# First sum over the edges: two products of constants behind every chunk's product on TensorE

## The reference, cut to what matters

```
agg = jax.ops.segment_sum(x[nbr], dst, num_segments=n)
cnt = jax.ops.segment_sum(jnp.ones((nbr.shape[0],), x.dtype), dst, num_segments=n)
mean = agg / jnp.maximum(cnt, 1.0)[:, None]
return x @ W1.T + b1 + mean @ W2.T + b2
```

## Time and profile before

| | us |
| --- | --- |
| median of 3 runs | 3077.75 (3067.9 to 3085.03) |
| the profiled execution: its own time | 3073.24 |
| its span, first to last instruction | 3071.5 |
| PE busy | 2177.0 (71%) |
| DVE busy | 1633.8 (53%) |
| ACT busy | 1448.1 (47%) |
| POOL busy | 1399.4 (46%) |
| mean granted clock of PE | 0.823 of full |
| the first sum's loop, first gather to last addition | 348.2 to 1034.0, some 22% of the span |

### The profile page before, as it was taken

The page is one execution under the profiler, slowest core; times in us unless marked ns, Lnnn a source line. Parts: engine busy times, 40 slices in busy tenths (PEclk is TensorE's granted clock), DMA queues, the critical chain, the costliest instruction groups (busy, mean ns, idle before and its releaser), DMA issues. The chain is left out here.

```text
span 3071.5 us, 60350 instructions
## 1 busy us (share of the span) xinstructions
PE 2177.0 (71%) x15045; PEld 1791.5 (58%) x15046; DVE 1633.8 (53%) x4124; ACT 1448.1 (47%) x3571; POOL 1399.4 (46%) x1397
## 2 busy tenths in 40 slices
PE   4889744445444589999657677777777598859991
PEld 3756432333332479999535566666666477639990
DVE  8899722222222643333455555655655787873436
ACT  6789622323232343433364444444444588643335
POOL 0000365656565223333135555555655199735550
PEclk9989966767676789999877777777887699979995
DMA  2300154323232511111315555555656288572223
GB/s 100 126 15 22 53 171 135 116 83 89 83 90 82 129 46 34 38 36 36 113 67 172 166 176 166 170 177 169 182 175 160 72 275 268 177 277 87 70 68 135
DMA packets 182513, 368.87 MB, mean 120 GB/s; under 512 B 30426, under 2 KB 67716, under 8 KB 182126
## 3 DMA queue, kind: packets, MB, share of 16 engines
q1 hardware_dynamic: 118489, 208.65, 20.0%
q0 software_dynamic: 53760, 148.67, 18.1%
q10 hardware_dynamic: 10133, 9.97, 1.0%
HBM read 275.35 MB, written 91.83 MB: 120 GB/s over the span
## 5 line engine op out<-in xcount | busy, mean ns | idle before, releaser
L830 POOL DMA_INDIRECT weightsL_w<-y_gnn,all_slot_dst x440 | 421.6, 958 | 408.1 <-PEq L899 158.4
L830 POOL DMA_INDIRECT scores_rows<-h_gnn,all_slot_dst x440 | 430.5, 978 | 370.3 <-ACT scores_ends L2131 230.5
L920 PE MATMUL sum_ps<-weightsL_w 128*128 128x256 f32 x880 | 316.8, 521 | 346.9 <-issue 218.2
L920 PEld LDWEIGHTS sum_ps<-weightsL_w 128*128 128x128 f32 x880 | 214.9, 260 | 448.8 <-issue 412.7
L935 DVE TENSOR_TENSOR sums_acc<-sums_acc,sum_ps 128x256 f32 x440 | 185.2, 421 | 479.6 <-remote 285.4
L2072 PE MATMUL scores_diff_ps<-scores_minus,scores_node 128*128 128x128 bf16 x2640 | 353.0, 247 | 67.7 <-issue 67.5
L2072 PEld LDWEIGHTS scores_diff_ps<-scores_minus,scores_node 128*128 128x128 bf16 x2640 | 289.6, 124 | 121.8 <-issue 96.1
L890 ACT ACTIVATE weightsL_w<-all_count_f,all_slot_src 128x128 f32<-128x128 f32 x440 | 133.8, 388 | 455.1 <-PEq L924 404.8
L1528 PE MATMUL expertsL_hid_ps<-sums_acc,expertsL_w 128*128 128x128 f32 x2816 | 335.9, 276 | 3.8 <-DVE sums_acc L1599 2.8
L1579 ACT ACTIVATE sums_acc<-expertsL_hid_ps,expertsL_b 128x128 f32<-128x128 f32 x704 | 197.6, 372 | 299.1 <-PE expertsL_hid_ps L1528 246.4
L1528 PEld LDWEIGHTS expertsL_hid_ps<-sums_acc,expertsL_w 128*128 128x128 f32 x2816 | 325.7, 193 | 4.4 <-issue 4.2
(11 more groups left out here) (436 smaller groups left out, 4302.0 us busy)
## 6 DMA issues: line engine op xcount, KB each, us to landing
saved_gnn<-scores_rows SPq DMA_DIRECT2D x220, 264.0 KB
sum_rows<-saved_gnn SPq DMA_DIRECT2D x220, 264.0 KB, 3.1
weightsL_w<-in_L_ffn_W SPq DMA_DIRECT2D x16, 1024.0 KB
weightsL_w<-in_L_ffn_w SPq DMA_DIRECT2D x32, 512.0 KB, 9.2
scores_lanes<-slot_lanes SPq DMA_DIRECT2D x44, 320.0 KB
sort_low_b<-low_lanes SPq DMA_DIRECT2D x32, 416.0 KB, 3.5
weightsL_w<-ys_L SPq DMA_DIRECT2D x6, 1280.0 KB, 11.6
weightsL_w<-y_gnn,all_slot_dst POOLq DMA_INDIRECT x440
```

The source lines that it names most:

```text
L830: pool.indirect_dma_start(out=self.rows[s] if isinstance(self.rows, list) else self.rows[:, s, :], out_offset=None, in_=table[:, :], in_of ...
L920: last = nc.tensor.matmul(ps[s % banks][:, 0:D], pick[h][:, s % HALF, :], g.rows[s], start=True, stop=True)
```

## The change

A further PSUM tensor of the stage, `idle_ps`, is made (the stage then holds eight: five for chunks, two for positions, and this one). Behind every chunk's product, and ahead of the wait at the end of a half, PE issues two products of constants of 512 columns each into it. No semaphore, no other engine and no DMA is touched. It is 880 products more, each with its weight load.

```
--- before.py
+++ after.py
@@ -858,6 +858,7 @@
         end_hot = m.sb("end_hot", [P, ENDS, P], FP16)
         end_chunk = m.sb("end_chunk", [P, ENDS, QP], FP16)
         within_ps, ends_ps = m.ps("within_ps"), m.ps("ends_ps")
+        idle_ps = m.ps("idle_ps")
         end_ready, end_placed, ends_kept = (m.sem(n) for n in ("end_ready", "end_placed", "ends_kept"))
         cleared = m.sem("cleared")
@@ -919,6 +920,7 @@
                         pe.sem_inc(tick, 1)
                         last = nc.tensor.matmul(ps[s % banks][:, 0:D], pick[h][:, s % HALF, :], g.rows[s], start=True, stop=True)
                         last.then_inc(summed, 1)
+                        idle_products(nc, c, idle_ps, 2)
                         if s % HALF == HALF - 1:
                             pe.wait_ge(summed, k + 1)
                             pe.sem_inc(g.freed, 1)
```

## The result

Over 14 runs each, the kernel with the constants takes 3058.52 us (3044.22 to 3069.85), the kernel before 3081.11 us (3067.9 to 3108.06). The ratio is **0.9922 [0.9897, 0.9948]**: 0.8% faster, where I had forecast 1.2% slower. The profiled execution's span is 3046.8 us against 3071.5, so 24.7 us less.

The account below looks back on a forecast made before the run. The prediction took the first sum to be bound by POOL's gathers plus its stops. 3073.2 + 36 for (a) + 4 for (b), with nothing for (c), gave 3113 us, range 3052 to 3165.

Parts of the forecast that it names:

- What bounds the stage: First sum: its time is POOL's gathers, 24.8 us per turn, plus 21 stops, 122.2 us in all.
- (a): First sum's loop: slower PE bursts give two POOL stops of 3.9 us per turn for one of 5.7: +36 us.
- The burst behind a restart: After POOL restarts, PE's ten chunks take 10.5 us against 7.5, past the 8 to 9 us of on-time words.
- The price of a stop: POOL's stop behind ten gathers: 3.5 us until words pass plus 0.4 for `freed`, 3.9 us; 42 make 164.
- a falling sum: POOL's stops on line 924: expected over 155 us in all; a fall in their sum would prove the forecast wrong.
- (b): First sum loop's end: the last ten chunks have no cover and take PE 10.7 us, not 6.54: +4 us.
- the bounds of (a): First sum's loop: at best 13 us more, 3090 with the end; at worst 69 us more, 3146.
- (c): PE's loop, four instructions longer per chunk, and the unread bank `idle_ps`: taken to cost nothing, at most 1.25 us per turn.
- The clock: PE in the first sum: a turn's granted clock rises from 0.67 to about 0.8.
- the faster rival: First sum's stop: PE at full clock has ten products ready, one 3.9 us stop per turn: 38 us saved, 3035; chance 0.11.

Follow-up runs that it names:

- e17: The changed kernel again, on a chip without late words, against the kernel before: 2752.13 us, ratio 1.0013.
- e10: Kernel before, no constants; POOL asks for free slots each five gathers and not each ten, by summed products: 3044.27 us, ratio 0.9825.
- e12: Kernel before, no constants; ahead of each ten gathers POOL waits for the eighth product of the ten chunks just gathered: 3077.67 us, ratio 0.9875.
- e13: Kernel before, no constants; one drain of PE behind each second product gives the words of two products: 3180.65 us, ratio 1.0212.
- e7: Kernel before, no constants; POOL waits ahead of each turn's eleventh gather for that turn's fifth product: 3077.37 us, ratio 0.9993.
- e2: The changed kernel with one product of constants per chunk in place of two, against the kernel before: 2756.58 us, ratio 1.0019.
- e16: The changed kernel with POOL also asking for free slots each five gathers, against the kernel before: 2748.82 us, ratio 1.0006.
- e8: Kernel before, no constants; ahead of each turn's first and eleventh gather POOL waits also for the product five chunks on: 3095.64 us, ratio 0.9982.
- e14: The changed kernel again, on a chip with late words, against the kernel before: 3069.09 us, ratio 0.9862.
- e5: The kernel before, unchanged, run once more for its profile: 3089.52 us (one run).
- e15: Kernel before, no constants, POOL asking for free slots each five gathers, on a chip without late words: 2747.18 us, ratio 0.9992.
- e4: Kernel before with each finished product's word given by a drain of PE behind it, on a chip without late words: 2905.06 us, ratio 1.0545.
- e9: Kernel before with each finished product's word given by a drain of PE, in the third group: 3121.72 us (one run, 0.8% over).

## Why the prediction was wrong

**What bounds the stage: right.** POOL's gathers (19.04 and 19.07 us busy per turn, with 0.3 us between them) plus its stops account for the loop, before and after.

**(a) The burst behind a restart: right.** Forecast 10.5 us with three chunks at half clock; measured 11.3 to the tenth product's end in the burst shown and 10.3 on average, with three at half clock and one across the rise. It passes the time in which words are on time, the tenth word is late, and POOL stops each ten gathers: 42 stops, forecast and found.

**(a) The price of a stop: this step failed.** The forecast carried "3.5 us until the late words are through", read behind twenty gathers, over to stops behind ten, and got 3.9 us each, 164 in all. It is 2.05 us + 0.33 us in the stop shown, 2.33 on average, and the 42 make 102.7 us with the first one. The prediction named a falling sum as a sign that it is wrong, and the sum fell. With 2.33 the same sum reads 42 × 2.33 = 98, less 6 and less 122.2: −30 us, and with (b) 3047; the profiled execution took 3048.48. (That it comes so close is partly luck: the first stop was 7.1 us and not 2.33, and (b) was some 5 us too high.) The profile of before had no steady stop behind ten gathers to read it from. The term that carried the forecast had only stops behind twenty under it, and the bounds of (a), 3090 to 3146, both took their 3.5 us as given. If the time for words to pass had been bounded below as well, by nothing, the range would have reached to the faster side for a reason.

**(b) The loop's end: wrong, and small.** Forecast +4 us. From the last gather's end to the last addition it is 13.8 us, against 14.4: the word passes after 2.0 us and not 3.5; PE's last stretch takes 10.1 us and not 8.3; and DVE, which had a backlog behind five banks' worth of late words before, ends 1.2 us behind PE and not 2.1. −1.5 + 1.8 − 0.9 = −0.6.

**(c) Code and PSUM: right**, at nothing. POOL's and ACT's busy times stand, and within a burst at full clock the chunks follow one another 0.87 us apart, which is what their products need.

**The clock: size right, and no gain by itself.** Forecast 0.8 for a turn, measured 0.84. The Trainium skill's page "TensorE: Matmul & The Clock Gate" (section "What's actually happening") says that activity releases the throttle, and the trace agrees: the clock rises in the fourth chunk of the burst, and a turn has 0.84 against 0.67. That this pays was the faster rival's rule. e17 (1.00, no gain) shows that it doesn't where no word is late, and e10 and e12 (0.70 and 0.59, gains of 1.75 and 1.25%) that it isn't needed where words are. What the clock does in the changed kernel is to pay for the constants: by the prediction's 1.7 us per chunk at half clock, ten chunks would take 17 us, and the stop behind ten gathers would last some 5 us and not 2.3. That is an estimate; no run had the constants without the clock.

**The rivals.** The faster one had the right side and the wrong mechanism. It asked for one stop of 3.9 us per turn with PE at full clock in it. In truth it is two of 2.3 us, and what held of it is that no product is left to make when the gathers end. That came from POOL stopping ten gathers earlier, and not from PE being quicker: PE needed 11.3 us for a half that took 7.5. I gave it 0.11, and the range reached down to 3052, so the measured 3058.52 lies in it, near its lower end. That is luck: no term of the sum and no bound of (a) leads under 3090.

**What stays open.** Why words are late while POOL gathers, on some chips and not on others, wasn't found; that it isn't the kind of instruction that gives them is what e13 says. Why more gathers make them pass later is open as well; 0.15 us per gather is a line through three points, and in four stops of e7, behind twenty gathers and with the product already done, POOL stood 4.1 to 4.2 us, which is above it. What the clock is worth beside late words, with nothing else changed, wasn't measured: e2 (one constant) and e16 ran only on chips without them. e10 and the changed kernel never ran on the same chip, so that e10 is the faster of the two rests on ratios from two chips (0.9825 [0.979, 0.986] against 0.9862 [0.9811, 0.9912] and 0.9944 [0.9909, 0.9979]) and on its shorter loop. On e8's to e14's chips no kernel before was profiled, so how much of the gains of 1.3 to 1.8% lies in the loop there is not known: against the loops' ends of before and e5 (1034.0 and 1031.9), on other chips, e12's loop is only 6 to 8 us shorter, where its median is 31 us lower.

## What to carry to other kernels

When a wait is released late by something that isn't an engine, its length belongs to the rhythm in which it was read. If a change alters the rhythm, the length has to be taken as unknown in both directions. More and shorter stops can be cheaper than fewer long ones, and an edit that only wastes an engine's time can bring that about; a wait put where it belongs (e10) gave at least as much, without the waste. Where no word is late, neither gains anything (e15, e17). And a busier engine at a higher clock is no gain by itself: look at the engine that bounds the stage.

## What the runs showed of the hardware that was not expected

- The same kernel before takes 2749 and 2754 us (medians) in two of the groups and 3081 to 3109 in the others, 12% more. In the first sum the difference is the late words: last addition at 915.4 to 921.2 us for e15 to e17, at 997.4 to 1034.0 in the same kernels and the kernel before where words are late. That is a part only: the changed kernel takes 306 us less on e17's chip (2752.13 against 3058.52), and 88 us of that lie in this loop; the rest wasn't looked into.
- A word from PE can reach DVE 8.4 us (e13) after it was due, with DVE, PE and the data ready, whether a product or a drain gives it. It passes 2.0, 2.9 or 3.5 us after POOL's gathers stop, behind 10, 15 and 20 of them (after, e10, before). Where PE worked close behind the gathers (e12) few words were late, on the same chip.
- With a drain behind each product a chunk takes PE 1.51 us at the low clock (e4, e9), against 0.85 for the product alone: 0.66 us each.
